# Edge tiles of 128 records in place of 125 in a fused graph kernel on one NeuronCore

## What is computed

```python
xn = layernorm(x)
x = x + gnn_attention(xn, src, dst, edge_type) + linear_attention_stack_of_4_layers(xn)
x = x + top2_of_16_experts(layernorm(x))
xn = layernorm(x)
x = x + gated_gnn(xn, ...) + linear_attention(xn)
x = x + ffn_of_the_top_half(layernorm(x))

# in gated_gnn, h is the batch-normed xn
a_in  = segment_sum((h @ W_in  + b_in )[src] * edge_weight[:, None],    dst)
a_out = segment_sum((h @ W_out + b_out)[dst] * edge_weight_n2[:, None], src)
```

## Time and profile before

| | us |
|---|---|
| median of 3 runs | 5154.09 (5144.35 to 5155.28) |
| span of the profiled execution | 5104.5 |
| PE busy | 4208.8 (82%) |
| DVE busy | 3215.8 (63%) |
| ACT busy | 2149.0 (42%) |
| POOL busy | 3136.1 (61%) |
| scatters (800) | 1684.5 |

### The profile page before, as it was taken

The page is one execution under the profiler, slowest core; times in us unless marked ns, Lnnn a source line. Parts: engine busy times, 40 slices in busy tenths (PEclk is TensorE's granted clock), DMA queues, the critical chain, the costliest instruction groups (busy, mean ns, idle before and its releaser), DMA issues. The chain is left out here.

```text
span 5104.5 us, 67642 instructions
## 1 busy us (share of the span) xinstructions
PE 4208.8 (82%) x19715; PEld 3144.9 (62%) x19715; DVE 3215.8 (63%) x6298; ACT 2149.0 (42%) x7759; POOL 3136.1 (61%) x2100
## 2 busy tenths in 40 slices
PE   6779689889786688888888788469983999999998
PEld 4567467667564466666666566345552788887566
DVE  7667376576386888888888688731114444444447
ACT  2732463473281466666666588312221222222122
POOL 2013388787788777777777688688876445443300
PEclk9989889989898798988888899769996999999999
DMA  9999832332233788888888344449984565563100
GB/s 301 294 336 321 268 67 38 42 63 37 28 61 53 223 265 266 264 267 265 265 266 253 70 94 94 111 105 289 292 246 143 218 236 222 219 234 128 39 15 26
DMA packets 758155, 896.70 MB, mean 176 GB/s; under 512 B 382262, under 2 KB 617430, under 8 KB 754514
## 3 DMA queue, kind: packets, MB, share of 16 engines
q1 hardware_dynamic: 327060, 611.62, 36.0%
q0 software_dynamic: 411376, 263.90, 23.8%
q10 hardware_dynamic: 19406, 17.44, 1.1%
HBM read 668.38 MB, written 222.64 MB: 175 GB/s over the span
## 5 line engine op out<-in xcount | busy, mean ns | idle before, releaser
L737 POOL DMA_INDIRECT pairs<-REC,FARC x800 | 1684.5, 2106 | 619.6 <-DMA pairs<-REC,FARC 231.1
L1102 PE MATMUL a_pa<-a_VW,identf 128*128 128x260 f32 x1760 | 551.3, 468 | 207.9 <-issue 114.2
L994 POOL DMA_INDIRECT a_KV<-kv_tab,KEYS x556 | 536.5, 965 | 173.6 <-issue 159.1
L1102 PEld LDWEIGHTS a_pa<-a_VW,identf 128*128 128x128 f32 x1760 | 389.3, 232 | 289.8 <-issue 121.4
L2664 DVE TENSOR_TENSOR AIN<-AIN,w_pin 128x512 f32<-128x512 f32 (+1 forms) x325 | 216.6, 666 | 374.2 <-PE w_pin L2701 374.0
L1065 ACT ACTIVATE a_VW<-a_KV,a_VW 128x64 f32<-128x64 f32 x1668 | 407.3, 334 | 2.7
L994 POOL DMA_INDIRECT XN<-kv_tab,KEYS x324 | 312.7, 965 | 98.7 <-issue 90.2
L2709 PE MATMUL w_pout<-XN,w_tT 128*128 128x256 f32 x1250 | 318.7, 379 | 0.0
L2678 ACT ACTIVATE w_tT<-w_pt 128x256 f32<-128x256 f32 (+1 forms) x300 | 117.4, 391 | 457.8 <-PE w_pt L2696 456.1
L2599 POOL TENSOR_TENSOR RES<-RES,REC 128x1600 f32<-128x1600 f32 x52 | 188.0, 3631 | 187.6 <-DMA REC<-pairs 187.4
L2599 POOL TENSOR_TENSOR HB<-HB,REC 128x1600 f32<-128x1600 f32 x48 | 174.2, 3642 | 181.4 <-DMA REC<-pairs 181.0
(11 more groups left out here) (661 smaller groups left out, 10066.9 us busy)
## 6 DMA issues: line engine op xcount, KB each, us to landing
pairs<-ZERO SPq DMA_DIRECT2D x32, 5000.0 KB, 46.5
e_W<-in_L_ffn_w SPq DMA_DIRECT2D x192, 512.0 KB, 6.0
REC<-pairs SPq DMA_DIRECT2D x100, 800.0 KB, 8.0
RES<-pairs SPq DMA_DIRECT2D x13, 3200.0 KB
HB<-pairs SPq DMA_DIRECT2D x12, 3200.0 KB, 10.3
m_crow<-cell_tab SPq DMA_DIRECT2D x71, 488.3 KB
row_tab<-a_arow SPq DMA_DIRECT2D x220, 130.0 KB, 4.4
a_tyb<-ty_tab SPq DMA_DIRECT2D x110, 256.0 KB, 7.0
```

Of the source, the lines that this page charges most:

```text
L737: pool.indirect_dma_start(self.pairs[half], bass.IndirectOffsetOnAxis(self.FARC[:, i:i + 1].bitcast(I32), 0), self.REC[:, i, 0:4].bitcast( ...
L994: pool.indirect_dma_start(KV[t % UB][:, j, :], None, self.kv_tab, bass.IndirectOffsetOnAxis(self.SIDX[:, t * ROW + j:t * ROW + j + 1], 0)) ...
L1102: last = pe.matmul(sums[t % NA], self.identf[:, :], VW[:, t % NV, e, :, :], start=e == 0, stop=e == ROW - 1)
```

## The change

A tile has 128 records. Partition p holds edges 781 p to 781 p + 780, and the 32 edges left over go to column 781, rows 0 to 31. So 782 columns are scattered (`EU`), and the buffers have 784 columns (`EC`), filled up with records of a cell outside the table and weight 0. The five loads are now on 128 partitions with 781 elements each, and five small ones (32 partitions, one element) follow; three of these and the later ones wait for the filling by DVE. The counting runs in 14 blocks of 2 x 28 columns in place of 10 of 2 x 40, and the steps between are tied to blocks 3, 4, 7 and 10. There are 98 groups of columns in place of 100; layers 1 and 2 have one group less, at their end. The cell rows are 512 bytes in place of 500. The written counts of scatters stay, so that `experts` gets 117 in place of 135. With 128 partitions the codes for the first of equal cells would leave the range of floats, so from partition to partition they fall by 8/3 and 3 in turn in place of 4; this changes constants only.

```diff
-EP = 125
-EC = E // EP
+EP = P
+EW = E // EP
+EU = -(-E // EP)
+EC = -(-EU // 8) * 8
+FARNODE, FARSRC = 4032, 3199
...
-BACKS = ((3, 3, 3, 3, 2), (3, 3, 3, 3, 3), (3, 3, 3, 3, 3), ())
+BACKS = ((3, 3, 3, 3, 2), (3, 3, 3, 3, 2), (3, 3, 3, 3, 2), ())
...
-        HC, HL, HH = 40, 64, N // 64 + 1
+        HC, HL, HH = 28, 64, N // 64 + 1
...
-                    pool.iota(CPI[:, :], pattern=[[1, 2]], base=249, channel_multiplier=-2).then_inc(s_io, 1)
+                    pool.iota(CPI[:, :], pattern=[[1, 2]], base=490, channel_multiplier=-3).then_inc(s_io, 1)
...
+                    for x, empty in ((DI, FARNODE), (SI, FARSRC), (TI, 0)):
+                        dve.memset(x[:, EW:], empty)
+                    dve.memset(WT[:, :, EW:], 0.0).then_inc(s_pad, 1)
...
-                    dve.wait_ge(s_in, 48)
+                    dve.wait_ge(s_in, 96)
...
-                        if b == 2:
+                        if b == 3:
...
-                        elif b == 3:
+                        elif b == 4:
...
-                        elif b == 5:
+                        elif b == 7:
...
-                        elif b == 7:
+                        elif b == 10:
...
                     for dst, x in ((DI, "dst"), (SI, "src"), (TI, "edge_type_64")):
-                        act.dma_start(dst[0:EP, 0:EC], a[x].rearrange("(p e) -> p e", p=EP)).then_inc(s_in, 16)
+                        act.dma_start(dst[:, 0:EW], a[x][0:EP * EW].rearrange("(p e) -> p e", p=EP)).then_inc(s_in, 16)
+                    act.wait_ge(s_pad, 1)
+                    for dst, x in ((DI, "dst"), (SI, "src"), (TI, "edge_type_64")):
+                        act.dma_start(dst[0:E - EP * EW, EW:EW + 1], a[x][EP * EW:].rearrange("(p e) -> p e", e=1)).then_inc(s_in, 16)
                     for w, x in enumerate(("edge_weight", "edge_weight_n2")):
-                        act.dma_start(WT[:, w, :], a[x].rearrange("(p e) -> p e", p=EP)).then_inc(s_pin, 16)
+                        act.dma_start(WT[:, w, 0:EW], a[x][0:EP * EW].rearrange("(p e) -> p e", p=EP)).then_inc(s_pin, 16)
+                        act.dma_start(WT[0:E - EP * EW, w, EW:EW + 1], a[x][EP * EW:].rearrange("(p e) -> p e", e=1)).then_inc(s_pin, 16)
...
-            if self.placed < EC:
+            if self.placed < EU:
...
-        LEFT = EC - self.placed - LAST
+        LEFT = EU - self.placed - LAST
```

More of the change, by code:

```diff
@@ L406, in open_up @@
         s_oh, s_hs, s_cnt, s_hd = (n(f"q_{x}") for x in ("oh", "hs", "cnt", "hd"))
-        s_p0, s_w1, s_p1, s_bo, s_own = (n(f"q_{x}") for x in ("p0", "w1", "p1", "bo", "own"))
+        s_p0, s_w1, s_p1, s_bo, s_own, s_pad = (n(f"q_{x}") for x in ("p0", "w1", "p1", "bo", "own", "pad"))
         s_cf, s_ct, s_cr, s_cd, s_park, s_rec = (n(f"q_{x}") for x in ("cf", "ct", "cr", "cd", "park", "rec"))
-        HC, HL, HH = 40, 64, N // 64 + 1
+        HC, HL, HH = 28, 64, N // 64 + 1
         NB = EC // (2 * HC)
@@ L456, in _ @@
                                        base=31, pattern=[[32, P // 32], [0, 32]], channel_multiplier=-1)
-                    pool.memset(self.REC[:, :, 7:8], 2.0 ** 121)
+                    pool.memset(self.REC[:, :, 7:8], 2.0 ** 119)
                     pool.memset(CNT[:, HH:], 0.0)
@@ L477, in _ @@
                     dve.wait_ge(s_io, 5)
-                    dve.tensor_scalar(CPI[:, :], CPI[:, :], 23, None, ALU.logical_shift_left)
+                    dve.tensor_scalar(CPI[:, :], CPI[:, :], 22, None, ALU.logical_shift_left)
                     for j in range(LOW):
@@ L482, in _ @@
                     dve.drain()
-                    dve.tensor_scalar(self.C2[:, :], CPI[:, 0:1].bitcast(F32), 1.5, None, ALU.mult).then_inc(s_cp, 1)
+                    dve.tensor_scalar(self.C2[:, :], CPI[:, 0:1].bitcast(F32), 2.0, None, ALU.mult).then_inc(s_cp, 1)
                     dve.tensor_scalar(SG[:, :], SGI[:, :], -2.0, 1.0, ALU.mult, ALU.add)
@@ L574, in _ @@
                     self.load_back(act, 0)
-                    act.wait_ge(s_pin, 32)
+                    act.wait_ge(s_pin, 64)
                     act.activation(parts[0], WT[:, :, :], ACT.Copy).then_inc(s_p0, 1)
@@ L2479, in _ @@
                 def _(pool):
-                    self.place_pairs(pool, EC - self.placed)
+                    self.place_pairs(pool, EU - self.placed)
                     self.wait_pairs(pool)
@@ L3017, in run @@
         self.ty_tab, self.dl_tab = self.dram("ty_tab", [P * SW], BF16), self.dram("dl_tab", [P * SW // ROW], BF16)
-        self.pairs, self.cell_tab = [self.dram(f"pairs{h}", [CELLS + E, 2]) for h in range(2)], self.dram("cell_tab", [EC, EP])
+        self.pairs, self.cell_tab = [self.dram(f"pairs{h}", [CELLS + EP * EC, 2]) for h in range(2)], self.dram("cell_tab", [EC, EP])
         self.xn_tab = self.dram("xn_tab", [NP, D])
@@ L3024, in run @@
         table = ExitStack()
-        RECS = self.sb(table, "REC", [P, EC, 8], BF16)
-        self.REC, self.FARC = RECS[0:EP, :, :], self.sb(table, "FARC", [EP, EC])
+        RECS = self.sb(table, "REC", [P, NP // 4, 8], BF16)
+        self.REC, self.FARC = RECS[:, 0:EC, :], self.sb(table, "FARC", [EP, EC])
         self.PART = RECS[:, :, :].rearrange("p e j -> p (e j)").bitcast(F32).rearrange("p (b n) -> p b n", b=2)
```

## The result

| | before | after |
|---|---|---|
| median, beside each other on one chip | 5152.97 us (4 runs) | 4974.34 us (4 runs, 4965.24 to 4980.63) |
| ratio | | 0.9664, 95% interval 0.9644 to 0.9685 |
| span of the profiled execution | 5104.5 | 4970.1 |
| PE / DVE / ACT / POOL busy | 4208.8 / 3215.8 / 2149.0 / 3136.1 | 4123.8 / 3198.7 / 2145.8 / 2745.6 |
| scatters: count, mean | 800, 2.11 us | 782, 1.65 us |

The account below looks back on a forecast made before the run. POOL was taken to pace experts and end layers 1 to 3, edge lists to delay the opening; opening -6, layer 1 -11, layer 2 -18, layer 3 -5, experts -27 sum to -67: 5154.1 to 5087 us, range 5060 to 5130.

Parts of the forecast that it names:

- What bounds the kernel: By stage: POOL paces experts, PE close behind; POOL ends layers 1 to 3 last; DVE awaits edge lists in open_up.
- The scatter's price: All stages with scatters: 128 records cost the same 2.0 us as 125, so the term is 0.
- a least duration off 2.00 us: Sign that the prediction is wrong: a scatter's shortest time differs from 2.00 us.
- rival C: Full scatters as cheap as gathers, 1.0 us; layers 2 and 3, route and experts gain more: 5065 us; chance 0.08.
- the main case: Whole kernel: all terms as forecast, -67 us, 5087 us; chance 0.60.
- Loads on 125 partitions: Layers 1 to 3: cell-row loads spread over 16 engines instead of five, cutting POOL's waits; layer 2 gains 18, layer 3 5.
- Rival A: Loads stay on few engines or cell rows are limited by their source: -29 us, about 5125; chance 0.15.
- The group fewer: End of layers 1 and 2: one merging group less saves 5 us in layer 1, some 3 in layer 2.
- Opening: open_up: edge lists let CELL start near 14 us, -8; 14 counting blocks cost +2; net -6, bounds -8 and +4.
- Experts: experts: 18 scatters fewer bring POOL below PE's 5.82 us a tile; stage near 396 us, gain 27.
- Rival B: experts is bound by the DMA engines: -8 us in place of -27, 5106; chance 0.09.
- The base: Whole kernel: median 49.6 us above the 5104.5 us span, taken as fixed; forecast is 5154.1 plus the span's change.

Follow-up runs that it names:

- a_rec125: The changed kernel with scatters taking only partitions 0 to 124, the last three partitions' records left out: 5039.8 us, ratio 0.9810 to the kernel before.
- b_pad128: The kernel before with each of its 800 scatters on 128 partitions, three of the records empty: 5032.2 us, ratio 0.9805.
- b_crow128: The kernel before with cell rows broadcast to 128 partitions and the counting in 16 blocks of 2 x 25 columns: 5081.4 us, ratio 0.9895.
- b_fewer: The kernel before with scatters on 128 partitions, without the last merging group of layers 1 and 2 and the last 16 columns: ratio 0.9847.
- b_all: The kernel before, 800 columns of 125 records, with scatters and cell rows on 128 partitions and edge lists loaded as 112 and 13: 5405.9 us, ratio 0.9796.
- a_again: The changed kernel unchanged, run again on a chip where every kernel's att_rows was slow: 5368.9 us, ratio 0.9734 to the kernel before.
- b_again: The kernel before, unchanged, profiled once more: span 5128.0 us, time 5129.7 us.

## Why the prediction was wrong

**What bounds the kernel** was read rightly: POOL at the end of layers 1 to 3, its waits behind the cell rows, POOL pacing `experts` with PE close behind, the edge lists in the opening. Each of the four was shown by a kernel that took it away.

**The scatter's price** is the step that failed. "The 125 records look already filled up to 128" explained 414 packets as 16 x (8 x 3 + 2). They are 16 x 25 + 16, as if each of the 16 engines' lists were as long as that of an engine that carries 125/5 records. Both readings fit one number, and the count on 125 records alone could not tell them apart; the 5 that the loads showed in the earlier trace rows, and the rule behind it, would have, applied to the scatter: 128/16 = 8 a list in place of 25. The term was 0 where it is -0.46 us, for 782 scatters. By a_rec125, which has everything but the cheap scatters, this is some 75 of the 112 us by which the forecast of 67 fell short of 179. The prediction named the sign itself: a least duration off 2.00 us. The price was bounded by -1.0 (rival C), whose chance was put at 0.08 and whose sum (-22 us beyond the main case) counted DVE as the next bound in layers 2 and 3, right, but left out the 5 us in project and the 4 in att_nodes, where POOL was thought covered. Taken alone, in b_pad128, the cheap scatters are worth 100 us (84 to 115 by the interval).

**Loads on 125 partitions**: right in mechanism and, for layer 2, in size (18 forecast, 20 to 25 in b_crow128); layer 3 5 forecast, 3 to 5; layer 1 6 forecast with the group's 5 left aside, 8 or 20, depending on which profile of the kernel before is taken. POOL's waits fell as forecast, from 65 to 10 us. Rival A falls.

**The group fewer**: 3 to 5 us forecast, 4.3 and 1.1 in b_fewer, which is too near to no change to confirm it.

**The merging's weight loads** were in no term. The prediction asked what the narrower tiles cost, not whether a full 128 is a case of its own for PE. They are 0.042 us a load, and 5 to 8 us in layer 1.

**Opening**: the lists came 10.5 us sooner, 8 forecast; the queue of ACT (its wait of 8.75 us behind the five-engine loads) was gone, so `q_ior` was no longer late. (`q_ior` got 30% narrower, 1792 columns in place of 2560, not 11.2%; the sum used the right factor of 0.7.) The blocks gave -5 in place of +2: the counting matmul was costed at 0.209 us and takes 0.177. Of these 5 us b_crow128 shows less than 1 with its 16 blocks; the rest (14 blocks, where the steps stand between them, 128 partitions) was not taken apart.

**Experts**: -36 in place of -27. The 26 us of waits are as forecast; the 11.5 us of PE's work, less at a granted clock of 0.99 in place of 0.96 now that PE hardly waits, were not. The count of scatters, from which alone the forecast took its gain here, is worth nothing that the runs can tell: 0.6 us between b_all and a_again. Rival B (DMA engines) falls: their share rose to 0.94 and PE runs nearly without waits.

**Batch_norm**: no term; of the +9.9 us, 8.0 are additions that collide with DVE. The question "what will a faster engine collide with" was not asked of POOL's last stage.

**The base**: 49.6 us were taken to lie outside the span, and 1.7 do. The profiled execution was a short one. Since a change was added to the median, this did no harm to a forecast of a difference, but it hides 45 of the 179 us: the stages account for 134, and b_again places 22 of its 23.5 us of greater length in layers 0 and 1. Whether the change also removes what makes these two vary is open (the changed kernel's layer 0 was 391 to 414 us, of the kernel before 412 and 422).

## What to carry to other kernels

Let the partition count of a DMA, and of POOL's scatters above all, have 16 as a divisor, even where some rows are empty: three rows of padding in 800 scatters were worth 100 us here. (Gathers had 128 rows in all kernels, so for them this was not tried.) When a packet count has two explanations, look for a second row that tells them apart before the price is taken from it. Fill the weights of small bf16 matmuls up to 128 columns, which made each load 42 ns shorter. When an engine gets faster, look also at the stage after its last wait: its next work starts sooner and may meet DVE.

## What the runs showed of the hardware

- An accumulating scatter of r records takes POOL about 1.35 us + 1.65 ns x 16 r/k, with k the largest divisor of r up to 16: 1.55 us for 128 records, 1.61 for 120 and 126, 1.99 for 125, 2.22 for 124, 4.33 for 113, 4.69 for 127. Fewer records at k = 16 save little: 1.48 us for 112, 1.33 for 32 (the formula is up to 0.1 us off there).
- A bf16 weight load of 128 columns takes 96 ns and one of 125 columns 138 ns, at the same row stride and with 125 contraction rows; the small matmuls follow each other after 0.166 in place of 0.196 us.
- Counting matmuls of the same size take 0.209 us with 80 bytes between weights, 0.177 to 0.179 with 50 or 56 bytes.
- SP's loads of 0.5 MB broadcast to 125 partitions kept 4.4 of the 16 DMA engines busy and POOL's scatters waiting behind them, 65 us in three layers; broadcast to 128 partitions, POOL waits 8 us in the same layers (b_crow128).
- A product on DVE of 0.42 us takes up to 3.8 us if it starts while POOL adds two tiles of SBUF.
